# Third attention layer: row maximum taken straight over the PSUM bank, exponential reading the scores from PSUM

## The reference

```python
# L2, 8 query heads, 1 key/value head, head width 64, S = 512
h = ada_rms(x, time_emb, ln1_w, ln1_tw)
q = (h @ Wq.T).reshape(b, s, 8, 64).transpose(0, 2, 1, 3)
k = (h @ Wk.T).reshape(b, s, 1, 64).transpose(0, 2, 1, 3)
v = (h @ Wv.T).reshape(b, s, 1, 64).transpose(0, 2, 1, 3)
q = apply_rope(q, pos_ids)
k = apply_rope(k, pos_ids)
scores = jnp.einsum('bkgsd,bktd->bkgst', qg, k) / jnp.sqrt(64.)
attn = jax.nn.softmax(scores, axis=-1)
ctx = jnp.einsum('bkgst,bktd->bkgsd', attn, v)
x = res + ctx @ Wo.T
```

## Time and profile before

| | us |
|---|---|
| median of 3 runs | 2983.79 |
| lowest, highest | 2979.62, 2985.05 |
| span of the profiled execution | 2973.1 |
| TensorE, VectorE, ScalarE, GpSimd busy in it | 2498.1, 1685.8, 1242.6, 945.5 |
| attention of L2, first to last score tile | 1767.8 to 2119.3 |

### The profile page before, as it was taken

How to read it: one execution, slowest core, us unless ns; L and a number is a source line. 1 busy time by engine, 2 the same in 40 slices (tenths; PEclk the granted TensorE clock), 3 DMA queues, 4 the chain that set the end, 5 groups by cost and what they waited for, 6 DMA issues and landing times. The chain is left out here.

```text
span 2973.1 us, 49050 instructions
## 1 busy us (share of the span) xinstructions
PE 2498.1 (84%) x16368; PEld 2035.7 (68%) x16368; DVE 1685.8 (57%) x4627; ACT 1242.6 (42%) x2856; POOL 945.5 (32%) x982
## 2 busy tenths in 40 slices
PE   5879789788589999698788848889879999996787
PEld 4767677676478887576656537767668888885565
DVE  2777776677653443557675656576453333333866
ACT  1565565566421111556666636556441111112443
POOL 0233233243366666123233302233202112120422
PEclk8989899899799999678778969989989999997888
DMA  5000000000200100200000000000010010001000
GB/s 207 18 2 1 9 2 9 1 2 8 86 15 29 43 0 0 78 30 1 2 1 1 1 33 1 1 0 1 21 44 22 22 43 21 0 0 46 1 28 29
DMA packets 15747, 63.81 MB, mean 21 GB/s; under 512 B 2589, under 2 KB 2845, under 8 KB 10549
## 3 DMA queue, kind: packets, MB, share of 16 engines
q1 hardware_dynamic: 15540, 61.24, 5.7%
HBM read 57.00 MB, written 4.23 MB: 21 GB/s over the span
## 5 line engine op out<-in xcount | busy, mean ns | idle before, releaser
L777 ACT ACTIVATE l0a_prob<-l0a_prob,l0a_nmin 128x512 f32<-128x512 f32 x256 | 185.7, 726 | 199.8 <-DVE l0a_nmin L1031 199.6
L1553 POOL TENSOR_TENSOR l2m_hidl<-l2m_hid,l2m_hidh 128x512 fp32r<-128x512 f32 x64 | 100.8, 1575 | 482.5 <-DVE l2m_hidh L1529 482.5
L1195 POOL TENSOR_TENSOR l0a_prob<-l0a_prob,l0a_rinv 128x512 f32<-128x512 f32 x64 | 66.7, 1042 | 524.1 <-DVE l0a_rinv L1038 524.1
L1421 ACT ACTIVATE l2m_gate<-l2m_psG 128x512 f32<-128x512 f32 x64 | 38.3, 598 | 452.7 <-PE l2m_psU L1362 452.7
L1524 DVE TENSOR_TENSOR l2m_hid<-l2m_gate,l2m_psU 128x512 f32<-128x512 f32 x64 | 44.0, 688 | 300.1 <-ACT l2m_gate L1421 300.1
L777 ACT ACTIVATE l1a_prob<-l1a_prob,l1a_nmin 128x128 f32<-128x128 f32 (+3 forms) x256 | 143.2, 560 | 89.3 <-DVE l1a_nmin L1031 87.4
L644 PE MATMUL l0a_psT<-res_ident,l0a_prob 128*128 128x128 f32 x1024 | 167.0, 288 | 11.5 <-ACT l0a_PT L787 11.4
L1031 DVE CUSTOM_DVE_ANT_0 l0a_prob<-l0a_psS,l0a_mask 128x512 f32<-128x512 f32 x256 | 173.2, 687 | 2.6 <-issue 1.6
L1572 POOL TENSOR_TENSOR res_X<-res_X,l0m_share 128x512 f32<-128x512 f32 x128 | 162.3, 1295 | 26.2 <-DVE l0m_share L1513 25.0
L644 PE MATMUL l1a_psT<-res_ident,l1a_prob 128*128 128x128 f32 x640 | 134.5, 314 | 37.2 <-ACT l1a_PT L787 34.7
L1425 ACT ACTIVATE l0m_hid<-l0m_psG,l0m_b1c 128x512 f32<-128x512 f32 x64 | 44.2, 690 | 286.8 <-PE l0m_psG L1362 283.6
(11 more groups left out here) (374 smaller groups left out, 7859.7 us busy)
## 6 DMA issues: line engine op xcount, KB each, us to landing
l2m_stage<-in_l2m_w SPq DMA_DIRECT2D x8, 1536.0 KB, 6.9
l0m_stage<-in_l0m_w SPq DMA_DIRECT2D x8, 1024.0 KB, 4.8
cond_w<-in_wmod SPq DMA_DIRECT2D x6, 1024.0 KB, 5.9
res_X<-in_x SPq DMA_DIRECT2D x4, 1024.0 KB, 11.6
l0a_prob<-in_l0a_w SPq DMA_DIRECT2D x4, 1024.0 KB, 6.6
l1a_wmod<-in_wmod SPq DMA_DIRECT2D x4, 1024.0 KB, 5.3
out<-res_X SPq DMA_DIRECT2D x4, 1024.0 KB, 4.3
l_stage<-in_l_w SPq DMA_DIRECT2D x3, 1024.0 KB, 7.0
```

Source lines behind the costliest of these rows:

```text
L777: act.activation(prob[:, n % NP, 0:w], src[:, 0:w], ACT.Exp, bias=nmin[:, n % NP:n % NP + 1], scale=-1.0, accum_out=ssum[:, n % NP:n % NP ...
L1195: op = pool.tensor_tensor(x, x, r.to_broadcast([P, w]), ALU.mult)
L1553: pool.tensor_tensor(hidl[:, s % 2, m, :], hid[:, m, :], f32(hidh[:, s % 2, m, :]), ALU.subtract).then_inc(hl_done, 1)
```

## The change

In L2 alone DVE no longer writes the scores to SBUF: it takes the maximum over the PSUM bank, negated, with a plain reduction, and the memset of `beat` goes. ACT's exponential reads the scores from the PSUM bank and writes `prob` for the first time. So the bank is in use until the exponential is done, and `scores(n)` waits for `exp_done` of tile n-2 where it waited for `min_done`. The wait for the `prob` slot moves from DVE to ACT, and DVE waits instead until `nmin`'s cell has been read. The other two layers do what they did.

```diff
@@ PE, scores(b, n, first)
                     if n >= since(n) or not first:
-                        pe.wait_ge(min_done, b * NTILE + (n - since(n) + 1))
+                        pe.wait_ge(exp_done if is2 else min_done, b * NTILE + (n - since(n) + 1))
@@ ACT
-                def exps(b, n):
+                def exps(b, n, first):
                     w = P * L.nkeys[n // 4 % NT]
                     act.wait_ge(min_done, b * NTILE + (n + 1))
+                    if is2:
+                        if not (first and n < NP):
+                            act.wait_ge(pT_mm, b * NTILE + (n - NP + 1))
+                        act.activation(prob[:, n % NP, 0:w], psS[s_bank(n)][:, 0:w], ACT.Exp,
+                                       bias=nmin[:, n % NP:n % NP + 1],
+                                       accum_out=ssum[:, n % NP:n % NP + 1]).then_inc(exp_done, 1)
+                        return
                     src = prob[:, n % NP, :]
@@ DVE, minima(b, n, first)
                     v.wait_ge(s_done, b * NTILE + (n + 1))
+                    if is2:
+                        if not (first and n < NP):
+                            v.wait_ge(exp_done, b * NTILE + (n - NP + 1))
+                        v.tensor_reduce(nmin[:, n % NP:n % NP + 1], psS[s_bank(n)][:, 0:w], AX.X, ALU.max,
+                                        negate=True).then_inc(min_done, 1)
+                        return
                     if not (first and n < NP):
                         v.wait_ge(pT_mm, b * NTILE + (n - NP + 1))
-                    other = mask[:, qt, 0:w] if L.masked else R.zero[:, 0:1].to_broadcast([P, w])
+                    other = mask[:, qt, 0:w]
                     v.memset(beat[:, n % NP:n % NP + 1], 0.0)
```

More of the change, by code:

```diff
@@ L803, in batch @@
                         if n < NTILE:
-                            exps(b, n)
+                            exps(b, n, first)
                         if copy and (m - CL) % 4 == 0:
```

## The result

The changed kernel's median is 2988.74 us over 17 runs, that of the kernel before 2980.16 over 17 runs beside it. The ratio is 1.0026, 95% interval 1.0016 to 1.0036: **7.7 us slower** (4.8 to 10.7); the two medians differ by 8.6. The time itself came within 1.0 us of the forecast, and that was luck: I started from a median of three runs that was 3.6 us high, which hid most of a step of 8.6 where +3.9 was forecast. Read either way, the step is about twice the forecast.

A forecast was written before the change was run, and what follows sets the result against it. DVE or PE was taken to bound L2's attention, by stretch. Losses 1.4 + 4.1 less gains 1.2 and 0.4 make +3.9 us, so 2983.8 becomes 2987.7 us, 0.13% slower; 8-in-10 range 2981 to 2997.

The forecast's parts named there:

- What bounds the stage: L2's attention: DVE bounds tiles 0 to 13 of a batch; PE bounds the projections and the last batch's quiet second half.
- The reduction at 0.69 us, the exponential at 0.69: Per tile in L2: DVE's plain reduction 0.69 us (bounds 427 ns and 0.80 us), ACT's exponential from PSUM 690 ns.
- DVE's relief, 0.03 us a tile, 1.2 us: The dropped memset gains DVE 0.03 us on 14 tiles in each of three batches, 1.2 us; ends 0 and 6.0.
- The shorter exponential ... 0.4 us: ACT's exponential reading PSUM takes 0.03 us off each of the dozen waits that bind, 0.4 us gained.
- The bank comes free 0.85 us later at the least: Each L2 score bank is held until the exponential of tile n-2 is done, some 0.87 us after that exponential's start.
- The last batch, 4.1 us lost: PE's score waits: 0.74, 1.02, 0.85 and 0.75 us in the quiet tiles, 0.75 in the first half; ends 2 and 8.
- 3 x 0.47 = 1.4 us lost: Openings of the first three batches: late scores of tiles 2 to 4 reach DVE, which feels 0.47 us each time.
- In the stretches where PE projects, the bank is free 2 to 7 us early: cost nothing: In stretches with PE projections between the tiles, the projection itself covers the longer bank hold; loss nothing.
- The base: The median lies 10.7 us above the profiled span of 2973.1 us; this was added to the forecast span of 2977.0.
- Rival A: Idle pieces in the last batch's quiet half drop PE's clock to 1.2 GHz: some 10 us more, 2998 us; chance 0.11.
- Rival B: In DVE-bound stretches four late groups per batch each pass on 0.85 us: 10.2 in place of 1.4, 2996.5 us; chance 0.15.
- Rival C: DVE's relief counts in full, 0.142 us on 42 tiles: 2983 us; chance of a gain over 6 us 0.06.

The follow-up runs named there:

- hold_psum_exp: The changed kernel, but in L2 DVE keeps memset and custom operation, whose output in `prob` the exponential overwrites; stage 360.19 us, ratio 1.0044 to the kernel before.
- the two hold runs: Kernel before with only the score matmul's wait changed to the exponential, stage 360.59 us; the same with the exponential reading PSUM, 360.19 us.
- the hold alone: Kernel before with one edit: in L2 the score matmul waits for the exponential of tile n-2, not the minimum; stage 360.59 us, ratio 1.0029.

## Why the prediction was right or wrong

- **What bounds the stage**: right. Three kinds of stretch; the projections waited for no bank (what their beginning lost by the clock stands below), the quiet half of the last batch lost most for its length.
- **The reduction at 0.69 us, the exponential at 0.69**: right, 685 and 692 ns. The Trainium skill, VectorE: DVE Perf Modes, section on the TRN2 errata, would have had 43 ns off the exponential, an estimate from its cycle counts; the trace has 723 - 692 = 31.
- **DVE's relief, 0.03 us a tile, 1.2 us**: right per tile (0.40 us in 14). In the table tiles 4 to 13 give 1.1 back, but 0.4 of that also comes in the third batch of hold_psum_exp, which has no relief on DVE; against that run these 27 tiles give 0.7 us, again 0.03 a tile. By the end of the third batch only 0.17 us of it is left, as told above.
- **"The shorter exponential ... 0.4 us"**: right, 0.4 by the two hold runs.
- **"The bank comes free 0.85 us later at the least"**, with the start of a score matmul at the exponential's start plus 0.87: right, 0.83 and 0.84.
- **The last batch, 4.1 us lost**: right in mechanism and nearly in size. The four quiet terms were 0.74, 1.02, 0.85 and 0.75 and came as 0.74, 0.94, 0.76 and 0.66, the last three less by 0.08 or 0.09. The first half was to lose 0.75 and lost 1.3.
- **"3 x 0.47 = 1.4 us lost"**: mis-sized. It was 2.3. The product with V passed on all of the lateness of tile 3's scores: I had let 0.85 us reach tile 4's, and it was 1.05. The first batch, whose table load I had named, lost less than the others.
- **What fails is the sentence "In the stretches where PE projects, the bank is free 2 to 7 us early: cost nothing"**. True of the bank, but PE enters the first of these at half clock, and there it stayed for about five matmuls more. The term that was put at nothing measured +2.0 us at tiles 13 to 16, in two batches, of which 0.4 net came back. The kernel before with its transposes first pays it too, so it isn't the hold alone that brings it; why the clock came back later was not tried and stays open. I had looked for the clock only in the last batch.
- **The base.** I took the 10.7 us between span and median for what lies around the instructions. The changed kernel's profiled execution took 2990.75 us for a span of 2988.6, so what lies around is 2.2 us; the one profiled before was a short execution.
- **Rival A, the clock in the last batch**: did not come in the changed kernel, as the clock of that half was 1.00 with an idle piece of 0.45 to 1.07 us in each group. The Trainium skill, TensorE: Matmul & The Clock Gate, section A second HAM failure mode: psum-queue depth-cycling, has the clock swing under small idles of this kind; the trace doesn't show it in that half. It was nearer than it looks: with the hold alone the clock of the same batch did fall to 0.50, at tile 11, behind idle pieces of 1.10 and 0.58 us, and cost 1.2 us. **Rival B**, late banks coming through DVE's cover, is right at its place and wrong in number: DVE does stand idle for a late bank before its maximum, once in each of the first three batches, not four times. **Rival C** fell.
- **The sum**: +3.9 for 7.2 to 7.7. The ratio lies just over the 0.2% that was to part no change (0.63) from slower (0.31), and its interval reaches to both sides.

## What to carry to other kernels

Before a reader of a PSUM bank is moved to a later engine, count the ring: with two banks the bank's next writer waits for the whole chain scores, maximum, exponential, accumulator read-out, and what is lost is that chain less the work that the writer has in between. Compare start times tile by tile in the stretch where the writing engine is the bound, and add what stands behind it in order; saving instructions on an engine with slack buys nothing there. Try the semaphore's new condition alone in the old kernel first: here this one line showed 9.4 us of stage, where the whole change cost 7.5. And read the granted clock beside every difference of a microsecond: 1.2 us of these 9.4 were the clock and not the wait.

## What was not expected of the hardware

The stage came out within 0.2 us in two executions, while whole executions of the same kernel lie between 2975.46 and 2988.42 us, with differences of several us ahead of the stage. A change of a few us is better read in its stage's profile than in the total, if the stage has one clear beginning and end.

Small delays came together with a lower clock and grew. A delay of about 1.8 us at the start of a batch became 3.8 us of stage, with the granted clock at 0.52 from 1973 to 1980 us, the level of 1.2 GHz; with a shift of 1 us at tile 13, five more matmuls took about 0.63 us for 0.40. Both came where PE had just been idle, 1.98 us and 3.38 us. Much shorter idle pieces can go either way: 1.10 and 0.58 us came before a clock of 0.50 with the hold alone, and 1.07 and 0.29 us before a clock of 1.00 at the same tiles of the changed kernel, whose quiet groups, with pieces of 0.45 to 1.07 us, kept 1.00 as well.
